# Second attention and down projection in one block, split products in the last stage, key pool loaded in pieces

## The reference

```
x = x + attention2(cached_attention(x))
x = x + ffn(mix(x))
cached_attention: q, k, v = x Wq, x Wk, x Wv (32 query heads, 8 key heads, 128 wide); RMS norm and rotation of q and k;
                  keys and values of 16 pages a sequence out of a pool of 64 pages, and the own 32; softmax; times Wo
attention2:       q, k, v = y Wqkv; causal softmax over the 32 own tokens; times w_dense (the down projection)
mix:              x2 mixed within a sequence by one of 32 matrices of 32 x 32, chosen by index
ffn:              y W_base + bias, and 8 experts of rank 16: logits = y W_gate, the two best, softmax over them,
                  sum over the experts of weight * (y A_e) B_e
```

## Time and profile before

| | |
|---|---|
| median of 3 runs | 3167.01 us (3165.92 to 3167.49) |
| the profiled execution | 3165.54 us, of which the span from first to last instruction 3164.0 us |
| PE busy | 3063.2 us, 97% |
| DVE, ACT, POOL busy | 1818.8, 1497.6, 576.2 us |
| mean granted clock of PE | 0.987 |

### The profile page before, as it was taken

How to read it: one execution, slowest core, us unless ns; L and a number is a source line. 1 busy time by engine, 2 the same in 40 slices (tenths; PEclk the granted TensorE clock), 3 DMA queues, 4 the chain that set the end, 5 groups by cost and what they waited for, 6 DMA issues and landing times. The chain is left out here.

```text
span 3164.0 us, 92903 instructions
## 1 busy us (share of the span) xinstructions
PE 3063.2 (97%) x36400; PEld 2387.2 (75%) x36400; DVE 1818.8 (57%) x3389; ACT 1497.6 (47%) x3680; POOL 576.2 (18%) x1409
## 2 busy tenths in 40 slices
PE   8999999899999999999999999898999997899999
PEld 6888887767777777777777888777888886788884
DVE  5656668468888888888875444422333332444423
ACT  4555555367777777777774222122333333222210
POOL 0000001044555554455550000000000000300000
PEclk9999999999999999999999999999999999999999
DMA  5333333467676666777666443223333333643301
GB/s 202 99 109 93 113 93 94 161 189 213 209 218 208 212 212 213 210 214 214 210 212 197 122 120 109 76 105 130 100 98 113 98 96 96 195 120 120 94 26 53
DMA packets 504105, 456.01 MB, mean 144 GB/s; under 512 B 33778, under 2 KB 468466, under 8 KB 498547
## 3 DMA queue, kind: packets, MB, share of 16 engines
q1 hardware_dynamic: 471538, 367.06, 38.1%
q0 software_dynamic: 32256, 84.27, 8.4%
HBM read 321.10 MB, written 130.02 MB: 143 GB/s over the span
## 5 line engine op out<-in xcount | busy, mean ns | idle before, releaser
L808 PEld LDWEIGHTS ps_o<-weights_t,v_all 32*128 32x128 f32 x17408 | 509.1, 187 | 107.9 <-issue 107.9
L808 PE MATMUL ps_o<-weights_t,v_all 32*128 32x128 f32 x17408 | 557.7, 276 | 3.6 <-ACT o_t L708 1.8
L792 PE MATMUL ps_scores<-k_slot,q_slot 128*32 128x288 f32 (+1 forms) x8192 | 525.9, 397 | 6.8 <-PEq L96 4.7
L697 ACT ACTIVATE probs<-masked,shift 128x544 f32<-128x544 f32 x512 | 382.9, 748 | 245.0 <-DVE shift L743 243.2
L743 DVE CUSTOM_DVE_ANT_0 masked<-ps_scores,reach,scale_now 128x544 f32<-128x544 f32 x512 | 390.1, 762 | 171.5 <-PE ps_scores L792 167.6
L792 PEld LDWEIGHTS ps_scores<-k_slot,q_slot 128*32 128x32 f32 x8192 | 241.9, 110 | 200.2 <-issue 9.0
L756 DVE STREAM_TRANSPOSE weights_t<-probs 128x544 f32<-128x544 f32 x512 | 376.8, 736 | 23.7 <-ACT probs L702 10.5
L702 ACT ACTIVATE probs<-probs,inv 128x544 f32<-128x544 f32 x512 | 375.9, 734 | 0.0
L904 ACT ACTIVATE s_h_hi<-s_h_raw 128x2048 fp32r<-128x2048 f32 x64 | 122.9, 1920 | 525.3 <-PE s_ps L60 520.1
L84 POOL COPY k_slot<-k_pool 128x256 f32 x1024 | 359.0, 410 | 31.2 <-DMA k_pool<-kpool_in 16.7
L956 DVE TENSOR_TENSOR y<-y,s_ps 128x512 f32<-128x512 f32 x240 | 148.9, 683 | 354.3 <-PE s_ps L60 354.3
(11 more groups left out here) (164 smaller groups left out, 4676.3 us busy)
## 6 DMA issues: line engine op xcount, KB each, us to landing
v_all<-vpool_in SPq DMA_DIRECT2D x1024, 128.0 KB, 3.0
qT_scratch<-turned SPq DMA_DIRECT2D x64, 512.0 KB, 3.2
q_slot<-qT_scratch POOLq DMA_DIRECT2D x64, 512.0 KB, 3.5
oT_scratch<-o_t POOLq DMA_DIRECT2D x128, 256.0 KB, 5.0
s_h_raw<-oT_scratch SPq DMA_DIRECT2D x32, 1024.0 KB, 5.7
aT_scratch<-s_o_t SPq DMA_DIRECT2D x32, 1024.0 KB, 5.6
s_h_raw<-aT_scratch SPq DMA_DIRECT2D x32, 1024.0 KB, 5.7
w_raw<-w_in SPq DMA_DIRECT2D x12, 1024.0 KB, 6.1
```

The costliest lines, as they stand in the source:

```text
L697: act.activation(probs[:, k % BUF, :], masked[:, k % 2, :], ACT.Exp, bias=shift[:, k % BUF:k % BUF + 1], scale=-1.0, accum_out=total[:, k ...
L792: m = pe.matmul(ps_scores[q * S:(q + 1) * S, k % 2, cols], q_slots[j][:, head, r * S:(r + 1) * S], k_slots[j][:, pages, head * PSIZE:(head ...
L808: m = pe.matmul(ps_o[:, q, 0:GS], v_all[rows, j, t, e * D:(e + 1) * D], weights_t[rows, g, :, t * S:(t + 1) * S], start=t == 0, stop=t == NPP)
```

## The change

1. **Key pool.** Quarters 1 and 2 are loaded in 8 pieces of 256 KB each. Those of quarter 1 are issued behind the k stores of units 1 to 4 of the last k block, those of quarter 2 behind the first four v stores.
2. **Stages 4 and 5 share a block.** The first weights of stage 5 are loaded at the start of stage 4, the heads of its first units from unit 28 on, and these are split by ACT and DVE between their softmax steps. PE does three of the four parts of down projection unit 0 after the last scores, before the last values, and the fourth behind them. SBUF and PSUM tiles are placed so that this can be: unit 0 uses the banks of the projections and scores and one that was free, unit 1 those of the values. The residual is loaded in four 1 MB DMAs from POOL's queue after the last projection; the mix loads follow on that queue.
3. **Stage 6 with split products.** The gate, base and lb products are split products. wb, wga and lb are split in the last head group of stage 5 (`high_parts` on ACT: three copies; `low_parts` on DVE: three subtractions); the mixed y gets its high part from ACT and its low part from DVE out of PSUM, hw after its transpose likewise. Output banks are the four of `ps_y`. The `gate` follows two tiles behind, hw comes in four quarters, four `base` go ahead of the loop, and in the loop `base(t + 3)`, the lb product of t and then the transpose of t + 2 are issued.

```diff
@@ stage1, sync @@
-            def load_pool(part):
+            def load_pool(part, piece, pieces):
...
             def block_of(i, cb, kind, pool_part=None):
...
                     sp.dma_start(dst, src).then_inc(store_free[u % 2], 16)
+                    if pool_part and 1 <= u <= 4:
+                        if u == 1:
+                            sp.wait_ge(q_scale_done, SEQ * G * 2)
+                        for k in range(2):
+                            load_pool(pool_part, 2 * u - 2 + k, POOL_PIECES)
...
-            for cb in range(2):
-                block_of(4, cb, "k")
-            sp.wait_ge(q_scale_done, SEQ * G * 2)
-            load_pool(1)
+            block_of(4, 0, "k")
+            block_of(4, 1, "k", pool_part=1)
             sp.wait_ge(rotated, RU + 1)
-            load_pool(2)
             for u in range(UN):
                 store_v(u, 1, UN + u + 1)
+                if u < 4:
+                    for k in range(2):
+                        load_pool(2, 2 * u + k, POOL_PIECES)
@@ over_heads @@
     def sync(sp):
-        load_w(0, 0)
-        load_h(0, 0, 0)
-        load_h(0, 1, 1)
+        if not seam:
+            sp.wait_ge(cached["k_gathered"], B)
+            load_w(sp, 0, 0)
+            load_h(sp, 0, 0, 0)
+            load_h(sp, 0, 1, 1)
+        load_w(sp, 1, 1)
         if loads:
             loads(sp)
-        load_w(1, 1)
...
-                if not (last and k >= UN - 2):
+                if not (last and k >= UN - 2) and not (seam and first and k == 0):
...
+    def first_low(dve):
+        dve.sem_inc(bank_free, 2)
+        w_low(dve, 0, 0)
+        h_low(dve, 0, 0)
...
+    def unit(pe, i, k, parts=range(4)):
+        n = i * UN + k
+        w, s = k // NT, k % 2
+        if parts[0] == 0:
+            if k % NT == 0:
+                pe.wait_ge(w_lo_done, i * 2 + k // NT + 1)
+            pe.wait_ge(h_lo_done, n + 1)
+            pe.wait_ge(bank_free, n + 1)
+        for j in parts:
+            if isinstance(n, int) and (n, j) in bank_ready:
+                pe.wait_ge(*bank_ready[n, j])
...
@@ stage4 @@
-            sp.dma_start(residual[0][:, :, :], a["x"].rearrange("(t p) n -> p t n", p=P)).then_inc(residual[1], 16)
+            heads["load_w"](sp, 0, 0)
...
+                    if last and k == UN - 1:
+                        sp.wait_ge(heads["h_lo_done"], 1)
+                        heads["load_h"](sp, 0, 2, 0)
                     sp.wait_ge(o_free, n + 2)
...
+                    if last and NT <= k < NT + 2:
+                        sp.wait_ge(w_lo_done, HK)
+                        sp.wait_ge(store_free[k % 2], 32)
+                        heads["load_h"](sp, 0, k - NT, k - NT)
...
+                    if last and k == NT:
+                        for g in range(G):
+                            heads["first_w_high"](act, g)
                     if not (last and k == UN - 1):
                         copies(n + 1, k + 1, range(1, PJ))
+                    if last and k >= UN - 2:
+                        heads["h_high"](act, 0, k - (UN - 2))
                     act.wait_ge(pv_done, n + 1)
...
+                    if last and k == UN - 2:
+                        heads["first_low"](dve)
...
                     if more:
                         project(n + 1, k + 1, i * 2 + (k + 1) // NT, range(PJ))
+                    else:
+                        heads["unit"](pe, 0, 0, range(3))
...
                     if more:
                         score(n + 1, 1 - s)
+                    else:
+                        heads["unit"](pe, 0, 0, range(3, 4))
@@ stage6 @@
-                act.activation(y_t[:, t, :], ps_y[:, t % 2, :], ACT.Copy).then_inc(y_copied, 1)
+                act.activation(y_high[:, t, :], ps_y[:, t % 4, :], ACT.Copy).then_inc(y_hi_done, 1)
...
+            for t in range(TILES):
+                dve.wait_ge(y_hi_done, t + 1)
+                dve.tensor_tensor(y_low[:, t, :], ps_y[:, t % 4, :], y_high[:, t, :].bitcast(F32), ALU.subtract).then_inc(y_lo_done, 1)
+                if t >= 2:
+                    copy_g(t - 2)
...
+            for part in range(4):
+                tiles = slice(part * QUART, (part + 1) * QUART)
+                dve.tensor_tensor(hw[:, tiles, :].rearrange("p t (e r) -> p (t e) r", r=R),
...
+                if part < 2:
+                    low_of(part)
...
+            bias_of(0)
+            bias_of(1)
             for t in range(TILES):
-                step(dve.tensor_tensor(x2[:, t, :], x2[:, t, :], bias[:, :], ALU.add))
+                if t + 2 < TILES:
+                    low_of(t + 2)
+                    bias_of(t + 2)
+                dve.wait_ge(biased, t + 1)
                 dve.wait_ge(out_done, t + 1)
                 if t >= 2:
                     dve.wait_ge(stored[t % 2], 16 * (t // 2))
-                dve.tensor_tensor(done[:, t % 2, :], x2[:, t, :], out_bank(t), ALU.add).then_inc(added, 1)
+                dve.tensor_tensor(done[:, t % 2, :], x2[:, t, :], ps_y[:, t % 4, :], ALU.add).then_inc(added, 1)
...
-                    m = pe.matmul(ps_g[:, t % 2, 0:E + ER], y_t[:, t, k * P:(k + 1) * P], wga[:, k, :], start=(k == 0), stop=(k == KC - 1))
+                    m = split_product(pe, ps_g[:, t % 2, 0:E + ER], y_high[:, t, cols], y_low[:, t, cols],
+                                      wga[1][:, k, :], wga[2][:, k, :], k == 0, k == KC - 1)
...
             def base(t):
                 if t >= 4:
                     pe.wait_ge(added, t - 3)
                 for k in range(KC):
-                    pe.matmul(out_bank(t), y_t[:, t, k * P:(k + 1) * P], wb[:, k, :], start=(k == 0), stop=False)
+                    split_product(pe, ps_y[:, t % 4, :], y_high[:, t, cols], y_low[:, t, cols], wb[1][:, k, :], wb[2][:, k, :], k == 0, False)
...
+            for t in range(4):
+                base(t)
+            for t in range(2):
+                turn(t)
             for t in range(TILES):
-                if t == 0:
-                    pe.wait_ge(hw_done, 1)
-                pe.transpose(ps_t[:, t % 2, 0:P], hw[:, t, :], c["ident"][:, :]).then_inc(t_done, 1)
+                if 1 <= t and t + 3 < TILES:
+                    base(t + 3)
+                pe.wait_ge(hw_lo_done, t + 1)
+                split_product(pe, ps_y[:, t % 4, :], hw_hi[:, t % 2, :], hw_lo[:, t % 2, :], lb[1][:, :], lb[2][:, :],
+                              False, True).then_inc(out_done, 1)
                 if t + 2 < TILES:
-                    base(t + 2)
-                pe.wait_ge(t_copied, t + 1)
-                pe.matmul(out_bank(t), hw_t[:, t % 2, :], lb[:, :], start=False, stop=True).then_inc(out_done, 1)
+                    turn(t + 2)
@@ build @@
+            pool.wait_ge(seam["proj_done"], last)
+            for span in range(NT):
+                pool.dma_start(x2[:, span * 4:(span + 1) * 4, :], a["x"][span * SPAN:(span + 1) * SPAN, :].rearrange("(t p) n -> p t n", p=P)
+                               ).then_inc(x_loaded[span], 16)
+            pool.wait_ge(seam["o_free"], seam["units"] + 1)
...
+                           h_free=[(seam["proj_done"], last - NT * seam["projections"]), (seam["proj_done"], last)],
+                           bank_ready={(0, 3): (seam["soft_step"], (seam["units"] - 1) * seam["steps"] + 1), (1, 0): (seam["o_free"], seam["units"] + 1)})
```

More of the change, by code:

```diff
@@ L188, in _ @@
                 load_x(span)
-            def load_pool(part):
-                cols = slice(part * quarter, (part + 1) * quarter)
+            def load_pool(part, piece, pieces):
+                size = quarter // pieces
+                first = part * quarter + piece * size
+                cols = slice(first, first + size)
                 sp.dma_start(k_pool[:, cols], a["kpool"][:, cols]).then_inc(c["pool_loaded"], 16)
@@ L830, in stage2, with over_heads @@
                 k_gathered=k_gathered, o_store_free=o_store_free, shift_done=shift_done, o_copied=o_copied, pv_done=pv_done)
-def over_heads(nc, hold, name, tiles, w_in, heads, result, tokens_first, copies, ready=None, loads=None, beside=None, cached=None):
+def over_heads(nc, hold, name, tiles, w_in, heads, result, tokens_first, copies, h_free, bank_ready, seam=False, ready=None, loads=None,
+               cached=None, high_parts=None, low_parts=None):
     w_raw, w_hi, w_lo, h_raw, h_hi, h_lo, ps = (tiles[k] for k in ("w_raw", "w_hi", "w_lo", "h_raw", "h_hi", "h_lo", "ps"))
@@ L1126, in stage4, with sync @@
         LAST = HK // 2 - 1
-        @block.sync
-        def _(sp):
+        def sync(sp, heads):
             for k in range(2):
@@ L1167, in split_w, with copies @@
                 act.activation(w_hi[:, slot, :, :], w_raw[:, :, :], ACT.Copy).then_inc(w_hi_done, 1)
-            def copies(n, k, heads):
-                for r in heads:
+            def copies(n, k, parts):
+                for r in parts:
                     act.wait_ge(proj_done, n * PJ + r + 1)
@@ L1202, in _, with vector @@
             groups(LAST, True)
-        @block.vector
-        def _(dve):
```

(21 more changed lines are left out.)

356 lines of the change are left out of this document (190 added, 166 removed).

## The result

The changed kernel takes **3177.39 us** (median of 13 runs, 3175.55 to 3180.48) against 3169.47 us for the kernel before, run beside it: ratio 1.0025, 95% interval 1.0016 to 1.0034, so slower by about a quarter of a per cent. The forecast was 3180.1. In the profiled executions the span went from 3164.0 to 3175.9 us, +11.9 against the forecast's +13.1. By the medians the change costs 7.9 us: the profiled execution of the kernel before was one of its faster ones, and the two traces, one execution each, don't show where its median loses the other 4.

A forecast was written before the change was run, and what follows sets the result against it. PE, busy for 97% of the span, was taken to bound the kernel. 3164.0 - 7.2 - 24.0 + 29.3 + 15.0 = 3177.1 us of span, plus 1.5 and another 1.5, gave 3180.1 us; range 3152 to 3190.

The forecast's parts named there:

- Part 1: Key pool in pieces, end of stage 1: PE's idle time and low clock go, gain 7.2 us, bounds 5.6 to 8.5.
- Part 2: Seam of stages 4 and 5: gain 26.3 us less 2.3 of stall, net 24 us, bounds 19 and 27.
- I take 2.3 us of stall, bounds 0 and 5: Behind the seam: PE waits 2.3 us before down projection unit 3 for its heads, h(3), landing between 2704 and 2707.
- Part 3: Gate products in stage 6: 192 fp32r matmuls at 0.229 us replace 14.7 us of f32 ones, +29.3 us.
- 0.229, what every 512-column fp32r matmul takes: Gate products: price in us taken for each 136-column fp32r matmul, where 0.057 and 0.1145 were the other bounds.
- rival (a): Gate: a narrow fp32r matmul costs one f32 weight load, +7.3 us in place of +29.3, kernel 3158.1 us; chance 0.27.
- Part 4: Output products in stage 6: period 5.6 us a tile against 4.41, +15.0 us, bounds +12 and +19.
- the ring: Output phase: base(t+3) waits for the add of tile t-1, queued on DVE behind work for t+1; period 5.6 us.
- rival (d): Output phase: no ring, adds arrive in time, 3.55 us a tile, tail 63.5 us, kernel 3151 us; chance 0.03.
- the clock stays up in the ring: Output phase: eleven periods take 61.6 us at 5.6 each; low clock costs 1.7 us only behind the lead-in's idle time.
- rival (c): Output phase: the clock falls in the ring, five of 12 gaps costing 1.7 us each, adding 9: 3189; chance 0.07.
- the gate spacing is below 0.16: Gate phase of the profile after: the sign, in us between gate matmuls, by which the forecast fails first.

The follow-up runs named there:

- experiment 3: Changed kernel with SyncE issuing the load of h(3) right behind the last store of attention: 3167.84 us, 9.6 faster than the changed kernel.
- experiment 5: Changed kernel with only the gate's products back in fp32, from a second unrounded copy by ACT: 3172.65 us, 4.7 faster than the changed kernel.
- experiment 4: Changed kernel with the last stage as in the kernel before, key pool pieces and seam kept: 3141.74 us, ratio 0.9915 to the kernel before.
- experiment 1: Changed kernel with TensorE two tiles ahead in the output phase, not three: 3136.35 us, 41.0 faster than the changed kernel.
- experiment 2: Changed kernel with DVE adding tile t before the low part and bias of tile t+2, three-tile lead kept: 3152.39 us, 25.0 faster.
- experiment 7: Changed kernel with the key pool's two quarters in one load each again, at their old places: 3186.38 us, 9.0 slower than the changed kernel.
- experiment 9: Changed kernel with two tiles ahead in the output phase, h(3) loaded earlier and the gate's products in fp32: 3118.52 us, ratio 0.9835.

## Why the forecast came out

**Part 1 was right**, in cause and size: 7.2 forecast, 7.2 between the two traces, 7.5 by undoing it inside one stage.

**Part 2: the seam was right, the load behind it mis-sized.** Less the 7.2 of part 1, the steps said 2666.4 for the first product, 2676.1 for the values and 2680.0 for unit 1; the trace has 2666.48, 2676.45 and 2680.4. The step that failed is "I take 2.3 us of stall, bounds 0 and 5" for h(3): it was 8.6 us, and with the low clock behind it 10.9 (experiment 3), so the part ended under its bounds of 19 and 27. Two terms made it. The store before it took 7.2 us to land, not 5.6, so SyncE went on at 2687.03 and not at 2685.0. And I let the 4.8 MB go at 316 to 410 GB/s, the rates of the earlier trace rows; from 2687.0 to 2706.4 they went at 4.8 MB/19.4 us = 247 GB/s. In that stretch all DMAs of the core together moved 305 GB/s, with the DMA share at 1.00: the rates of the rows are those of all queues, and SyncE's loads had only a part of it. POOL's gathers of the mixing matrices ran beside them; what they cost was not tried. Against this stands a gain that I did not see at all, 3.4 us in the rest of stage 5 (last section): -25.9 + 8.6 + 2.3 - 3.4 = -18.4, against -18.5 measured.

**Part 3: the step "0.229, what every 512-column fp32r matmul takes" failed,** and rival (a) holds. The reading "as if an fp32r product paid both loads of its f32 counterpart" rested on 0.229 being twice 0.1145, which was a coincidence of the widths: narrow products take 0.1115 us, 272 columns 0.127, 512 columns 0.227 to 0.229. The equal load durations of both kinds in the earlier trace rows were the better evidence, and I set them aside. By the measured price the term is 192 x 0.1115 - 14.7 = +6.7, and putting the products back gave 6.1 (experiment 5) and 6.5 (37.4 less the 30.9 of experiment 4). The rest of the +8.1, some 1.5 us, is a term that the forecast put at nothing: the clock is at 0.62 behind the idle time ahead of the phase, and the fp32 gate of experiment 4 pays 1.6 us for it too. Why the same idle time left it at 1.00 in the kernel before stays open. By the Trainium skill, "TensorE: Matmul & The Clock Gate", section "LDWEIGHTS (loading the stationary operand)", a weight load takes its columns divided by 1.2 GHz, an estimate of 107 ns for 128 columns. The trace's 0.1115 us a product, with PEld busy for all of 3036.2 to 3069, agrees with that within 5%.

**Part 4: the ring was right, its clock mis-sized.** The lead-in came out at 16.53 us (16.5 forecast), the undisturbed period at 5.7 (5.6), and experiments 1 and 2 show that the ring is the cause: open it and the phase takes 64.2 us (63.5 was rival (d)'s figure), shorten it by the two DVE operations and it takes 79.8. The step that failed is that the clock stays up in the ring. I had one row for it, where 1.88 us of idle time left it at 1.00, and gave rival (c) 7 in 100. It was low in eight of the eleven turns, which cost 2.3 us in the first (1.7 were forecast there) and 1.6 in each of the other seven. The 11 periods took 76.3 us, where 61.6 + 1.7 were forecast: 13.0 of the 14.5 us by which the part was too cheap; the other 1.5 lie behind base(15), where 14.0 us were measured and 12.5 forecast. The 29.5 are above the bound of 19. One row of a single gap did not carry over to a gap that comes back in every turn.

**The sum.** Part 3 was 21.2 us too dear, part 4 14.5 and part 2 5.5 too cheap, so the total is 1.2 us off in span by luck. Rivals (a) and (c) both came true, the one priced at 3158 and the other at 9 us on top, and neither case alone was the result. By its own sign the forecast failed: the gate spacing is below 0.16. The rule that the change costs time only above 0.161 us a product failed with it, since it cost time at 0.1115; and case (a) with seam and ring at their worse bounds is 3158.1 + 5 + 4 = 3167.1, no gain at all, not the 3164 that the chances went by.

## What to carry to other kernels

When a change lets an engine run further ahead, write down for each new buffer whose reuse it waits for, and what stands in the queue ahead of that release: here a third tile of lead closed a ring and cost 42.6 us, and one less gave it all back. A rate read from a window is that of all queues: a load gets what the others leave. At a seam, issue first the load that is wanted first and can't be hidden, ahead of loads that have hundreds of us. Splitting fp32 products into three fp32r ones paid for 512 columns (0.86 us against 0.69 a product; without the ring, 64.2 us from base(0) to the end against 77.3) and not for 136 (0.23 against 0.33).

## What the runs showed that was not expected

**The clock falls under a repeated short wait.** With 1.89 us idle in each turn of the ring it stood at 0.83 from 3093.6 to 3161.9, low in seven turns of ten, where 0.73 us in each turn left it at 1.00 from 3093 to 3145 (experiment 2). In each of the seven it cost 1.6 us, nearly as much as the wait. The length of a gap alone doesn't decide: 3.00 us ahead of the last stage left it at 1.00 in the kernel before, and 2.99 us at the same place put it at 0.62 in the changed one.

**Stage 5 runs 1% faster in the changed kernel.** Timeline of PE in its middle, 48 products apart:

```profile
2849.70 0.39 PE L58 MATMUL s_ps<-s_w_hi,s_h_hi 128*128 128x512 f32 x1
...
2860.58 0.39 PE L58 MATMUL s_ps<-s_w_hi,s_h_hi 128*128 128x512 f32 x1
```

That is 0.2267 us a product, at a granted clock of 1.00 as before, where the earlier trace rows give 0.2290: over 31 units of 48 products, 3.4 us. Experiments 3, 4, 7 and 9 have the same 0.2267 there. The change gives the tiles of the down projection other addresses in both memories; whether that is the cause was not tried and stays open.
